# The turn of the next batch's rows in the first attention: ten items in three heads of a batch in place of two

## What is computed

```python
xn = _layernorm(x, gamma_media, beta_media)      # context
ln = _layernorm(latents, gamma_lat, beta_lat)    # rows of x
q = ln @ Wq + bq
kv = jnp.concatenate([xn, ln], axis=1) @ Wkv + bkv
sim = jnp.einsum('bhid,bhjd->bhij', q, k)
attn = jax.nn.softmax(sim, axis=-1)
out = jnp.einsum('bhij,bhjd->bhid', attn, v)
return out.transpose(0, 2, 1, 3).reshape(b, -1, INNER) @ Wo + bo
```

## Time and profile before

| | us |
|---|---|
| median of 3 runs | 2563.03 |
| lowest, highest run | 2556.87, 2564.49 |
| the profiled execution | 2561.1 |
| its span, first to last instruction | 2559.4 |
| ScalarE, VectorE, GpSimd busy | 1899.9, 1921.2, 1818.0 |
| granted TensorE clock, mean of the span | 0.967 of full |

### The profile page before, as it was taken

One profiled execution on the slowest core, in us unless ns is written; L12 is line 12 of the kernel. 1 busy time (PEld: TensorE's weight loads), 2 busy tenths in 40 slices (PEclk: granted clock), 3 DMA queues, 4 the chain that ended last, 5 costly groups with the idle time before them and its releaser, 6 DMA issues. The chain is left out here.

```text
span 2559.4 us, 48371 instructions
## 1 busy us (share of the span) xinstructions
PE 2289.2 (89%) x16979; PEld 1395.7 (55%) x16980; DVE 1921.2 (75%) x3499; ACT 1899.9 (74%) x2979; POOL 1818.0 (71%) x1580
## 2 busy tenths in 40 slices
PE   5999999999999999999998589968888888689996
PEld 3454545444454445445554378835555555468775
DVE  7888778887778887878787556558989899666443
ACT  4787887878877878878888556538879789667554
POOL 2687877787777878777778477617878689556653
PEclk9999999999999999999999699989999999679998
DMA  5000000000000000000000375441202020375323
GB/s 151 1 1 1 27 1 1 1 1 1 27 1 1 1 1 1 1 1 1 1 1 1 106 174 146 97 111 32 60 20 61 11 52 2 126 195 127 49 43 64
DMA packets 90974, 108.66 MB, mean 42 GB/s; under 512 B 18866, under 2 KB 80259, under 8 KB 90707
## 3 DMA queue, kind: packets, MB, share of 16 engines
q1 hardware_dynamic: 68500, 80.57, 10.4%
q0 software_dynamic: 21696, 24.98, 6.3%
q10 hardware_dynamic: 544, 0.00, 0.0%
HBM read 68.75 MB, written 25.88 MB: 37 GB/s over the span
## 5 line engine op out<-in xcount | busy, mean ns | idle before, releaser
L432 POOL TENSOR_TENSOR a_acc<-a_acc,a_pf 128x512 f32<-128x512 f32 (+1 forms) x480 | 679.7, 1416 | 279.9 <-ACT a_pf L601 258.2
L906 DVE TENSOR_TENSOR a_pl<-a_pf,a_ph 128x512 f16<-128x512 f32 x448 | 470.7, 1060 | 23.5 <-ACT a_ph L607 23.5
L2218 POOL TENSOR_TENSOR c_pl<-c_pf,c_ph 128x512 f16<-128x512 f32 x320 | 377.0, 1207 | 118.1 <-ACT c_ph L2315 117.7
L601 ACT ACTIVATE a_pf<-a_psS 128x1024 f32<-128x1024 f32 (+1 forms) x288 | 280.8, 975 | 108.7 <-PE a_psS L624 102.5
L882 DVE TENSOR_REDUCE a_mx<-a_psA 128x1 f32<-128x512 f32 x504 | 330.7, 681 | 26.9 <-PE a_psA L681 25.4
L607 ACT ACTIVATE a_ph<-a_psS 128x1024 f16<-128x1024 f32 (+1 forms) x288 | 281.1, 976 | 0.0
L553 ACT ACTIVATE a_psS<-a_mb 128x1024 f32<-128x1024 f32 x255 | 248.7, 975 | 5.0
L1314 DVE TENSOR_TENSOR f_xn<-f_xn 128x256 f16<-128x256 f32 x312 | 129.6, 424 | 153.2 <-ACT f_xn L1283 126.1
L2551 DVE TENSOR_REDUCE c_wf<-c_psA 128x1 f32<-128x512 f32 x384 | 239.7, 679 | 6.3 <-PE c_psA L2387 5.2
L2308 ACT ACTIVATE c_pf<-c_psS 128x1024 f32<-128x1024 f32 x192 | 201.6, 1050 | 50.6 <-PE c_psS L2416 46.0
L1468 POOL DMA_INDIRECT f_sums<-f_xn,f_sidx x78 | 141.6, 1815 | 135.0 <-DVE f_xn L1867 108.4
(11 more groups left out here) (365 smaller groups left out, 6357.2 us busy)
## 6 DMA issues: line engine op xcount, KB each, us to landing
f_stage<-in_L_ffn_w SPq DMA_DIRECT2D x16, 1024.0 KB
f_stage<-in_L_ffn_W SPq DMA_DIRECT2D x16, 1024.0 KB
c_kst<-c_khs SPq DMA_DIRECT2D x64, 100.1 KB, 2.2
a_cx<-in_ctx SPq DMA_DIRECT2D x4, 1536.0 KB
c_cx<-in_ctx SPq DMA_DIRECT2D x12, 512.0 KB, 3.8
f_sums<-X SPq DMA_DIRECT2D x2, 2048.0 KB, 13.4
f_xrow<-f_xn SPq DMA_DIRECT2D x8, 512.0 KB, 4.8
c_kst<-c_kls SPq DMA_DIRECT2D x32, 100.1 KB, 2.2
```

The source lines that it names most:

```text
L432: g.tensor_tensor(acc[0:k, p, :], acc[0:k, p, :], pf[0:k, q % RF, i, :], ALU.add).then_inc(s_acc, 1)
L601: act.activation(pf[0:r, q % RF, 0:k, :], psS[q % 2][0:r, 0:k, :], ACT.Exp, scale=SCALE).then_inc(s_pF, 1)
L906: v.tensor_tensor(pl[0:r, q % RP, i, :], pf[0:r, q % RF, i, :], ph[0:r, q % RP, i, :], ALU.subtract).then_inc(s_pL, 1)
L2218: g.tensor_tensor(pl[0:r, q % RP, i, :], pf[0:r, q % RF, i, :], ph[0:r, q % RP, i, :], ALU.subtract).then_inc(s_pG, 1)
```

## The change

The ten T items of the next batch stood five in head 4 and five in head 5, at places (1, 2), (3, 3), (5, 0), (7, 2) and (8, 0). Now four stand in head 4 (items 2, 3, 0, 1, the last at (7, 2)), three in head 5 (4, 5, 6) and three in head 6 (7, 8, 9) at the first three places. Nobody uses (8, 0) any more, and only head 4 uses (7, 2). No instruction is added or taken away, and nothing else moves.

```diff
@@ -97,6 +97,7 @@
     TOP = U - 2
     SUM_AT = 2
     ON_POOL = {(4, 1), (5, 1), (6, 1)}
+    TURNS = {H0 - 4: (2, 3, 0, 1), H0 - 3: (4, 5, 6), H0 - 2: (7, 8, 9)}
...
-        if b + 1 < B and h in (H0 - 4, H0 - 3):
-            order = [2, 3, 4, 5, 6] if h == H0 - 4 else [7, 8, 9, 0, 1]
-            for (u, p), t in zip(((1, 2), (3, 3), (5, 0), (7, 2), (8, 0)), order):
+        if b + 1 < B and h in TURNS:
+            for (u, p), t in zip(((1, 2), (3, 3), (5, 0), (7, 2)), TURNS[h]):
                 at[u][p].append(("T", b + 1, t))
```

## The result

| | before | after |
|---|---|---|
| median, us | 2562.20 (20 runs, 2556.87 to 2566.84) | 2567.73 (20 runs, 2562.00 to 2575.01) |
| ratio | | 1.0023, 95% interval 1.0015 to 1.0030 |
| profiled execution, us | 2561.1, span 2559.4 | 2575.0, span 2573.3 |

So the change costs 3.8 to 7.7 us. That is real, but it lies within the 0.3% that was called no change. The profiled execution of after is the slowest of its twenty, and its span is 13.9 us longer, not 5.5. That is why the whole spans are not compared here, but the heads that the change touches.

What follows compares the result with a forecast made beforehand. TensorE was busiest (89%), T items priced by place, head 6's end set by GpSimd's chain. Per batch -0.16 + 0.35 + 1.67 = +1.86, three batches +5.6, on the median 2563.03: 2568.6 us; range 2561.5 to 2573.5.

Steps and rivals of the forecast that it cites:

- Head 4, -0.16: Head 4's tail: with (8, 0) empty, L700 can start 0.15 behind a_mrow, at 276.83 in place of 276.99.
- Head 5, +0.35: Head 5: middle stretch 21.83 in place of 20.61, emptied tail 7.79 in place of 8.66; sum 45.39 against 45.04.
- The tie in GpSimd's chain: Head 5: the chain may last 17.70 us before it is late, lasts 17.75 in head 4; charged at nothing.
- Head 6, +1.67: Head 6: chain starts at 23.18, lasts 17.19 plus 0.30, then 0.15 and 3.44; 44.26 against 42.59.
- The chain's new term: Head 6, GpSimd's chain to a_mrow: the new narrow subtraction was charged at 0.30 us.
- The bias is not added to the T item: Head 6's middle stretch: the bias's 0.66 is not added to the items' 1.20; 20.61, at worst 0.66 more.
- SP's later wait costs nothing: Queue SP: the next context load waits a head longer, about 45 us, but its first reader is over a head away.
- GpSimd becomes the bound: Rival, slower: GpSimd makes TensorE wait in head 5 from a chain of 17.70 us on; +8.7, 2571.7; chance 0.17.
- Placement does not matter: Rival: the T items' cost just moves with them between heads; 2563.0 us; chance 0.15.
- Balance pays: Rival, faster: waits of heads 4 and 5 come from load and go when spread; 8.5 in all, 2554.5; chance 0.06.
- the 0.66 that head 6 had over a bare head: Head 6's middle stretch in before: 20.07 against 19.41, from the output bias on GpSimd, 0.72.
- the narrow subtraction might keep VectorE out for 0.30 more: Head 6, shared port: right behind GpSimd's sums it could hold VectorE 0.30 longer; sum 0.9 higher, 6.5.

Runs made afterwards that it cites:

- e5: After, with T items moved from (1, 2) to (1, 3) and from (5, 0) to (4, 3); one run, 2551.71 us (before on that chip 2546.15).
- e2: After, with head 6's output bias moved from (6, 5) to (6, 2); one run, 2566.20 us (before on that chip 2566.43).
- e8: Before, with only the second biases of heads 6 and 7 moved to (6, 4) and (7, 4); 2539.63 us, ratio to before 0.9975.
- e3: After, with (5, 0) unused: four full items each in heads 4 and 5, two narrow in head 6's tail; 2560.18 us, ratio to before 0.9968.
- e1: After, with head 4's five items as before and head 6 without its full item at (1, 2); one run, 2567.63 us.
- e6: After, with (5, 0) unused, two full items in each tail of heads 4 to 6, biases at (6, 4) and (7, 4); 2531.19 us, ratio to before 0.9943.

## Why the prediction was right

2568.6 us was predicted and 2567.73 measured, against a median of before that came out 0.8 lower than the one shown. The difference, +5.6, was measured as +5.5.

- *Head 4, -0.16*: measured -0.15 (46.24). L700 again waits for `a_mrow`, 0.14 behind its end. Shown by the trace of after.
- *Head 5, +0.35*: measured +0.33. The two full items cost what they cost in head 4, 21.83. The tie in GpSimd's chain did not come up: it lasted 322.85 - 305.54 = 17.31, under the 17.70 that it might last. The 17.75 of head 4 was the wrong number for an odd head: `a_mrow` took 1.03 and not 1.49, since in head 5 VectorE's next `a_pl` starts 0.59 behind it and in head 4 0.52 ahead of it. With 1.49 it would have been 0.07 too late, so nothing hung on this. L700 did not wait.
- *Head 6, +1.67*: measured +1.63. Both waits and the chain came as forecast. Inside it the split was less good: the middle stretch took 20.48 (20.61 forecast), the tail 7.97 (7.88 was left for it). The chain's new term was off as well: the narrow subtraction took 0.76, not the 0.30 charged. The addition to `X` behind it took 1.41 for its pair where it had taken 1.86 in before, 0.45 less. In both kernels the first GpSimd operation behind those sums is the one held up by VectorE's `a_pl` (last section), so the length was paid once either way. The forecast did not say this; that its 0.30 fitted the chain is partly luck. That the sum held apart from that has a reason: the head was computed from GpSimd's chain, and what TensorE does in the middle stretch does not enter that. e5 bears it out with the same formula: 23.77 + 17.91 + 0.15 + 3.43 = 45.26, with a middle stretch 0.96 shorter.
- *The bias is not added to the T item*: right. The middle stretch took 20.48, not 21.27, and the V item of unit 6 no longer waits. The bias still costs its length in head 6, by way of GpSimd's chain, in after (e2) as in before (e8), where TensorE did its waiting for it in unit 6.
- *SP's later wait costs nothing*: right, by heads 7 and 0, which have not moved by over 0.03.

The rivals. *GpSimd becomes the bound* asked for a wait in head 5 and found none there. In head 6 it holds, as the forecast had it, and e5 shows it at work: 45.26. *Placement does not matter* is refuted by e3 against after: the same work is 0.32% faster than before at one set of places and 0.23% slower at another. *Balance pays* fell with the result, and spreading by count is no help: with four, three and three items the ratio is 1.0023, with four, four and two it is 0.9968. The Trainium skill (Perfetto Trace Analysis, Optimization Strategy) advises interleaving where the most contended engine changes over time. That condition is not met here, so the runs say nothing against it: in all nine stretches of heads 4 to 6 TensorE is the busiest engine. What TensorE waited for in heads 4 and 5 was not a loaded ScalarE but a buffer and a chain, and both are met again at the same places in the next head.

What the prediction missed besides changed nothing in its sum. It read the 0.66 that head 6 had over a bare head and took it as given; moving two biases by one unit each was worth about as much as the change cost: 4.0 us by the heads, 6.5 by the medians (e8).

## What to carry to other kernels

When work is moved in an order written out by hand, price it by the place and not by the piece: read bare, one-item and two-item stretches from the profile first, since here two narrow items cost 1.20 us at (3, 3) and (5, 0) of head 5, 0.57 at the same places of head 6, and 0.01 in the tail of head 6. A stretch that ends in a wait for another engine's chain is computed from that chain alone; shortening the rest only lengthens the wait, so the first thing to try is to take the small operations out of the chain and put them where its engine idles anyway. And a stretch that is above its bare length with no item in it is worth a look of its own.

## What the runs showed of the hardware

In the rows below, where VectorE's `a_pl` and a GpSimd operation meet, the one that starts first runs at its own length and the other is held up; 0.03 to 0.04 us decide. In e2, unit 2 of head 6, VectorE's low part `a_pl` and GpSimd's `a_sl` become ready together. The two engines, first in batch 0, then in batch 1 (head 6 starts at 325.00 and 672.23):

```profile
336.47 0.68 DVE L908 TENSOR_TENSOR a_pl<-a_pf,a_ph 128x512 f16<-128x512 f32 x1
...
336.50 1.66 POOL L440 TENSOR_TENSOR a_sl<-a_acc,a_sh 128x512 f16<-128x512 f32 x1
```

```profile
683.69 1.67 DVE L908 TENSOR_TENSOR a_pl<-a_pf,a_ph 128x512 f16<-128x512 f32 x1
...
683.65 1.17 POOL L440 TENSOR_TENSOR a_sl<-a_acc,a_sh 128x512 f16<-128x512 f32 x1
```

Where VectorE starts 0.03 earlier, its operation takes 0.68 and GpSimd's 1.66. Where GpSimd starts 0.04 earlier, they take 1.67 and 1.17. The later one is stretched by 0.49 where the other takes 0.68, and by 0.99 where the other takes 1.17: by somewhat less than the other's length. 683.65 + 1.17 = 684.82, and `a_pl` ends at 683.69 + 1.67 = 685.36, 0.54 behind, as it ended 0.55 behind GpSimd's sums in head 6 of before. The Trainium skill (SBUF — State Buffer, Who interferes with whom) has the shared pair as an exclusive lock; these rows agree but for 0.19 and 0.18 us, by which the later one is done sooner than behind a full lock. Three batches of one program, with the same instructions, thus differ by 0.8 us in that head. The prediction weighed that the narrow subtraction might keep VectorE out for 0.30 more in head 6. In after it went the other way round:

```profile
358.52 0.84 DVE L906 TENSOR_TENSOR a_pl<-a_pf,a_ph 128x512 f16<-128x512 f32 x1
...
358.77 0.76 POOL L413 TENSOR_TENSOR a_xtl<-a_tmp,a_xth 128x65 f16<-128x65 f32 x1
```

`a_pl` started late enough to lose only 0.16 to GpSimd's sums (356.20, 2.62; it ends 0.55 behind them), and then the narrow subtraction was held up, 0.76 in place of 0.30. In before it was the addition to `X` at the same point, 1.18 in place of 0.72.

The maxima's readings had one more face. The wait behind (5, 0) is 0.78 to 0.80 in every head where the item there is narrow (head 5 of before, head 6 of after, of e1 and of e2), and 0.41 where it is full, with two smaller waits about it (0.19 and 0.27 in head 5 of after). The prices are nearer to each other than the widths, but not the same: a full item at (5, 0) added 1.24 (e3), a narrow one 20.61 - 19.68 = 0.93 in head 5, by the stretch of e6 that has the narrow one at (3, 3) alone. At (3, 3) the width does count: 1.18 full, 19.68 - 19.41 = 0.27 narrow. The middle stretch of head 5 in e6:

```profile
294.10:313.78 19.68, 18.97 (x122) 10.28 (x121) 17.07 (x29) 15.76 (x25) 15.50 (x14) 1.00 0.00 1
```
